# Attention scores that contract 64 rows of the TensorE array in place of 128, with key buffers of half the size

## What is computed

```python
xn = layernorm(x)
x = x + L0_attn(xn) + L0_ffn(xn)    # attn: linear attention with Taylor features, and a sliding window of 64
xn = layernorm(x)
x = x + L1_attn(xn) + L1_ffn(xn)    # attn: causal softmax attention; ffn: 8 experts, each token goes to 2
```

## Time and profile before

| | |
|---|---|
| runs | 1350.98, 1356.68, 1357.42 us, median 1356.68 |
| profiled execution | 1351.23 us, of it 1349.2 us between the first and the last instruction |
| TensorE matmuls busy | 92% |
| DVE, ACT, POOL busy | 60%, 53%, 45% |
| granted TensorE clock, mean | 0.979 of full speed |

### The profile page before, as it was taken

One profiled execution on the slowest core, in us unless ns is written; L12 is line 12 of the kernel. 1 busy time (PEld: TensorE's weight loads), 2 busy tenths in 40 slices (PEclk: granted clock), 3 DMA queues, 4 the chain that ended last, 5 costly groups with the idle time before them and its releaser, 6 DMA issues. The chain is left out here.

```text
span 1349.2 us, 26273 instructions
## 1 busy us (share of the span) xinstructions
PE 1235.1 (92%) x9090; PEld 868.6 (64%) x9090; DVE 812.3 (60%) x3359; ACT 713.4 (53%) x1532; POOL 602.2 (45%) x793
## 2 busy tenths in 40 slices
PE   4998999999999999999999999999999837689997
PEld 2465576657765776577657765776577625389997
DVE  4065387638853886388538853885388448356663
ACT  2266267625772577257725772576257602457675
POOL 6133153515441544154425442544254533658787
PEclk9999999999999999999999999999999977889999
DMA  9403430243023302340234023402340034034443
GB/s 268 112 3 89 109 80 9 88 107 90 9 87 93 105 9 87 86 112 9 87 87 110 10 88 86 110 11 82 91 108 13 10 87 160 29 58 67 58 68 45
DMA packets 82227, 101.83 MB, mean 75 GB/s; under 512 B 12472, under 2 KB 43104, under 8 KB 82016
## 3 DMA queue, kind: packets, MB, share of 16 engines
q1 hardware_dynamic: 60160, 80.24, 22.1%
q0 software_dynamic: 14304, 10.61, 5.0%
q10 hardware_dynamic: 7632, 9.31, 2.2%
HBM read 55.44 MB, written 46.37 MB: 75 GB/s over the span
## 5 line engine op out<-in xcount | busy, mean ns | idle before, releaser
L955 ACT ACTIVATE probs<-bank 128x512 f32<-128x512 f32 (+2 forms) x896 | 441.7, 582 | 259.7 <-PE bank L578 254.6
L578 PE MATMUL bank<-K,Q 128*128 128x192 f32 (+4 forms) x1024 | 243.1, 317 | 15.0 <-issue 13.6
L1132 POOL TENSOR_SCALAR_AFFINE_SELECT probs<-probs 128x384 f32<-128x384 f32 x256 | 127.0, 518 | 282.5 <-ACT probs L955 281.4
L578 PE MATMUL bank<-Q,K 128*128 128x192 f32 (+4 forms) x1024 | 216.4, 318 | 2.9 <-DMA Q<-mrow_c 2.6
L635 PE MATMUL heads<-probs,V 128*9 128x192 f32 (+4 forms) x3072 | 196.1, 396 | 14.2 <-DVE probs L1375 5.6
L578 PEld LDWEIGHTS bank<-K,Q 128*128 128x128 f32 x1024 | 170.2, 193 | 42.6 <-issue 27.5
L578 PEld LDWEIGHTS bank<-Q,K 128*128 128x128 f32 x1024 | 150.9, 192 | 33.3 <-issue 19.0
L635 PEld LDWEIGHTS heads<-probs,V 128*9 128x9 f32 x3072 | 75.6, 91 | 125.8 <-issue 82.9
L945 ACT ACTIVATE probs<-bank,sh_s 128x512 f32<-128x512 f32 x64 | 44.0, 687 | 212.5 <-PE bank L571 201.8
L578 PE MATMUL bank<-QM,K 128*128 128x512 f32 (+3 forms) x512 | 137.6, 332 | 11.2 <-DVE mx_s L1323 6.3
L1186 POOL DMA_INDIRECT out<-h1T_s x78 | 122.8, 1574 | 46.6 <-issue 26.9
(11 more groups left out here) (190 smaller groups left out, 2061.9 us busy)
## 6 DMA issues: line engine op xcount, KB each, us to landing
Q<-slots_of_q SPq DMA_DIRECT2D x16, 1024.0 KB, 10.5
K<-slots_of_k SPq DMA_DIRECT2D x64, 192.0 KB
QM<-slots_of_qm SPq DMA_DIRECT2D x8, 1024.0 KB, 9.0
slots_of_q<-Q SPq DMA_DIRECT2D x24, 256.0 KB, 3.0
slots_of_k<-QM SPq DMA_DIRECT2D x24, 256.0 KB, 4.0
slots_of_qm<-Q SPq DMA_DIRECT2D x24, 256.0 KB, 4.2
slots_of_k<-Q SPq DMA_DIRECT2D x24, 256.0 KB, 3.0
slots_of_q<-Q ACTq DMA_DIRECT2D x24, 256.0 KB, 4.8
```

Of the source, the lines that this page charges most:

```text
L578: mm = pe.matmul(to[:, at:at + right.shape[1]], left, right, start=True, stop=True, skip_group_check=True)
L955: return act.activation(to, bank, func, scale=scale, bias=bias).then_inc(taken_sem(run, unit), 1)
L1132: pool.affine_select(out=three, in_=three, compare_op=ALU.is_ge, fill=0.0, base=0, pattern=[[0, 3], [1, P]], channel_multiplier=-1)
```

## The change

A score matmul takes 64 of the 128 partitions: rows 0 to 63 for heads with h % 4 of 0 or 1, rows 64 to 127 for 2 or 3. Within such a half only one neighbour head is left whose queries must be met by zero keys. So two heads, h and h + 2, can share a block of keys, one in each half, and there are eight blocks in place of sixteen. The number of matmuls, their columns, the bytes that the DMAs move and the order of the units stay as they were.

```diff
-        Q2, K2b = sb("Q2", [P, G, T], F32R), sb("K2", [P, H, T], F32R)
+        Q2, K2b = sb("Q2", [P, G, T], F32R), sb("K2", [P, H // 2, T], F32R)
...
-            Q1, QM, K1 = sb("Q1", [P, G, T], F32R, early), sb("QM", [P, G, T], F32R, early), sb("K1", [P, H, T], F32R, early)
+            Q1, QM, K1 = sb("Q1", [P, G, T], F32R, early), sb("QM", [P, G, T], F32R, early), sb("K1", [P, H // 2, T], F32R, early)
...
-                        sp.dma_start(to[ROWS * i:ROWS * i + 3 * D, i:H:HG, :].bitcast(F32), groups[i][0:3 * D]).then_inc(S[f"slots_{name}"], 16)
+                        sp.dma_start(to[ROWS * i:ROWS * i + 3 * D, i % 2:H // 2:2, :].bitcast(F32), groups[i][0:3 * D]).then_inc(S[f"slots_{name}"], 16)
...
+            def rows_of(h):
+
+                at = 2 * ROWS * (h % HG // 2)
+                return slice(at, at + 2 * ROWS)
+
             def q_part(buf, h, a, n):
-                return buf[:, h // HG, a:a + n]
+                return buf[rows_of(h), h // HG, a:a + n]
+
+            def k_part(buf, h, a, n):
+                return buf[rows_of(h), 2 * (h // HG) + h % 2, a:a + n]
...
-                    parts.append((WQ * (j % 2), q_part(Q1, h, P * j, P), K1[:, h, first:P * (j + 1)]))
+                    parts.append((WQ * (j % 2), q_part(Q1, h, P * j, P), k_part(K1, h, first, P * (j + 1) - first)))
...
-                    return at, keys[:, h, P * j:P * (j + 1)], q_part(buf, h, P * j, TRI_N[j])
+                    return at, k_part(keys, h, P * j, P), q_part(buf, h, P * j, TRI_N[j])
...
-            pool.memset(K1[:, H // 2:H, :].bitcast(F32), 0.0).then_inc(S["keys1_cleared"], 1)
+            pool.memset(K1[:, H // 4:H // 2, :].bitcast(F32), 0.0).then_inc(S["keys1_cleared"], 1)
...
-            dve.memset(K1[:, 0:H // 2, :].bitcast(F32), 0.0).then_inc(S["keys1_cleared"], 1)
+            dve.memset(K1[:, 0:H // 4, :].bitcast(F32), 0.0).then_inc(S["keys1_cleared"], 1)
```

More of the change, by code:

```diff
@@ L428, in set_keys @@
                     row = ROWS * i + 3 * D
-                    sp.dma_start(slots_to[name][row:row + D, i:H:HG, :].bitcast(F32), scratch[name].rearrange("(g i) r t -> i r g t", i=HG)[i][3 * D:4 * D])\
+                    sp.dma_start(slots_to[name][row:row + D, i % 2:H // 2:2, :].bitcast(F32), scratch[name].rearrange("(g i) r t -> i r g t", i=HG)[i][3 * D:4 * D])\
                         .then_inc(S["slots_set"], 16)
@@ L592, in part @@
                 def part(h, j, at):
-                    return at, q_part(Q2, h, P * j, P), K2b[:, h, 0:P * (j + 1)]
+                    return at, q_part(Q2, h, P * j, P), k_part(K2b, h, 0, P * (j + 1))
                 p, u = n // 5, n % 5
@@ L615, in slide_scores @@
                 for j in (2 * (n % 2), 2 * (n % 2) + 1):
-                    parts.append((WQ * (j % 2), K1[:, h, P * j:P * (j + 1)], q_part(Q1, h, P * j, SLIDE_N[j])))
+                    parts.append((WQ * (j % 2), k_part(K1, h, P * j, P), q_part(Q1, h, P * j, SLIDE_N[j])))
                 scores_into(run, SLIDE_UNITS[n], parts)
```

## The result

The changed kernel takes 1409.3 us (median of four runs, 1406.8 to 1412.4) against 1357.1 for the kernel before. The ratio is 1.0395, 95% interval 1.036 to 1.043. That is 52 us more where the prediction's sum said 21, and outside its range. The profiled execution took 1410.9 us; its span grew from 1349.2 to 1408.8 us. (That is 60 and not 52: the profiled execution of before was one of its shortest.)

What follows compares the result with a forecast made beforehand. TensorE sets the pace, with DVE close behind in pairs. Six steady batches at +3.1 us (18.6), last +1.9, first +0.5 and tail 0 make +21 on 1354: 1375 us; own range 1360 to 1390, 8 in 10 1342 to 1390.

Steps and rivals of the forecast that it cites:

- the prediction's sum: Whole kernel: +3.1 us per steady batch times six, last batch +1.9, first +0.5, tail 0; +21 us.
- A visit: Whole-array work inside half-row scores, there and back: two switches, taken as 0.35 us, bounds zero and 0.5.
- The slide part: Sliding maxima's transpose to dense: visits at 0.35 us less overlap and a DVE wait, slower by some +2.2 us.
- Its overlap: Slide: touching score units of different halves run side by side in 7 places, saving 0.8 of 7.2 us.
- The part before it: Third layer to the sliding maxima's transpose: 0 from 726.5 to 757 us; +1.2 us for 757 to 785.
- A switch of rows: Between whole-array work and half-row scores: 0.09 us for emptying and 0.10 for a load in the open.
- rival 1: Row switches are free and overlap stays: -1.9 us a batch, -14 over all, about 1341 us; chance 0.25.
- Rival 2: Half-row matmuls run as ordinary ones, neither overlap nor drain: time stays at 1352 to 1357 us; chance 0.12.
- rival 3: Drain without overlap, halves take turns: +4.8 us a batch, +33, about 1388 us; chance 0.07.
- rival 4: Half-array scores drop the clock to 1.2 GHz in pairs, doubling their 37.6 us: over +200 us; chance 0.03.
- Covers: Waits hiding other changes: halving K1's 3.47 us DVE clearing gains nothing, since TensorE's first matmul waits for a load until 10.05.
- From 726 to 757: Pairs stretch with five visits: +1.75 us against about -2 from overlap, taken as 0, bounds -0.8 and +1.

Runs made afterwards that it cites:

- the added matmul: Changed kernel plus one whole-array matmul of 512 columns per batch, before the first causal maximum unit's wait for queries: 1405.4 us.

## Why the prediction was wrong

**Without the clock its sum was nearly right.** It had +3.1 us for a steady batch; a batch at full clock measures +2.4 at most. A visit, put at 0.35 us, came out at 0.28 to 0.35. The slide part was put at some +2.2 (two visits of pairs included) and is +1.3. Its overlap, 1.0, came near what was laid out; its visits, some 3.3 in the sum, cost 2.3, the difference between 37.9 us without overlap and 35.56 before. Which visits hide behind a wait was not looked into. The part before it came to at most +0.8 with the added matmul in it, near what was laid out there. A switch of rows costs much as one of columns does, with the loader idle for 0.17 us and 0.21 us more to the next start, and rival 1 falls. The Trainium skill, TensorEngine Tiling (Array Packing), Tiling Modes, says that a change of tiling mode drains TensorE. The trace agrees with it by these two numbers. Rival 2 falls too (both mechanisms are seen), and so does rival 3: without overlap the kernel takes 1447, not 1409.

**The step that failed is rival 4, the clock.** The sum put a fall of the clock at nothing, and the prediction gave it a chance of 0.03, for two reasons, both bad. It called `weigh`, which holds full clock, evidence that a thinly used array is safe. But `weigh` lasts 2.3 us between scores that then used all rows, while the change thins the scores themselves, for nearly all of pairs. And it priced a fall as all or nothing, 37.6 us doubled in each batch. What came is 13.7 us of half clock in each of seven batches, at a price of 4.7 us. Work that runs for 13.7 us at half clock would take 6.8 at full clock; that a part of the loss was taken up in TensorE's waits is likely, but not shown. Why a score on fewer rows counts for less stays open.

**Where the 60 us of span went.** From the second third layer to the last, six batches, the distance grew from 817.7 to 859.9 us: +42.3, of which 6 times 2.4 = 14 at most are overlap and switches and 28 the clock. The first batch, with 20.5 us at half clock, is 6.7 longer. The last batch and the tail are 10.6 longer; of these 5.6 are pairs with its two falls. What the tail owes to the clock I did not separate. In sum, as an estimate, 17 to 20 us are the predicted mechanisms and some 40 the clock. The run with 65 rows, which has the clock's loss without the other two, cost 39.

**Covers held.** Clearing K1 on DVE took 1.76 in place of 3.47 us, and TensorE still began at 10.26 us, on the same load. Dense changed by 0.3 us. From 726 to 757 no gain could be read, since the half clock lies there.

## What to carry to other kernels

A matmul with fewer rows costs its full time (with 65 rows in every score the slide part takes 35.56 us, as with 128), and it can also cost the clock for everything that runs next. Before rows are cut from work that fills most of a stage, allow for that: full rows carried the clock here across waits, and 64 or 65 rows lost it even behind stretches in which TensorE was shown busy nearly all the time. Count the visits of whole-array work inside the part that is tiled, here about 0.3 us each, against the places where two tiles really touch, here 0.11 to 0.14 us each. And compare stage by stage, in batches of equal granted clock: here that split one 52 us result into two causes.

## What the runs showed of the hardware that was not expected

- With 65 rows in score matmuls and nothing else changed that shows in time, TensorE lost its clock behind stretches in which it was shown busier (2.49 of 3.42 us, and even 3.38 of 3.40) than in stretches through which the kernel before kept it (2.18 of 3.41, 2.15 of 3.40). The loss is graded: before the tail TensorE spent 20.5 us at half clock with 96 rows and 106 us with 65.
- Full rows don't protect the clock from waits: with another order of the units and all 128 rows TensorE spent 34 us at half clock before the tail.
- A matmul on 65 rows, from row 0, is ordinary work: its weights are loaded ahead right behind transposes. One on rows 0 to 63 is not: behind transposes the loader rests 0.17 us first, in the changed kernel and in the one where all heads use the lower half.
- The stretches at half clock of the changed kernel come at the same two places of each steady batch, 8.5 to 8.8 and 39.2 to 39.5 us after the third layer starts, and each lasts 6.8 us.
